# Sparsemax cross-attention and ffn on one core: three Newton rounds for the thresholds instead of four, members compared by row, and a rearranged end

## The chip, the cores and the metric

The kernel runs on one core of a Trainium2 chip. The time is that of the device, in microseconds; three runs of the kernel before gave 677.35, 680.38 and 681.27 us, median 680.38. One more execution was profiled; its trace is what is read here.

## What is computed

Eight batches of 100 queries and 722 context rows, model width 512, 16 heads of 32. The attention's weights are a sparsemax, not a softmax: in each row of scores a threshold tau is subtracted and what is negative is cut, with tau such that the rest sums to one.

```python
def sparsemax(x):
    x = x - max(x); zs = sort(x, descending)
    cssv = cumsum(zs) - 1.0
    k = count(zs > cssv / rho)                 # rho = 1, 2, ...
    tau = cssv[k - 1] / k
    return clip(x - tau, 0.0)

q, k, v = layernorm(x) @ Wq + bq, ctx @ Wk + bk, ctx @ Wv + bv      # 16 heads each
attn = sparsemax(q @ k.T * 32 ** -0.5)                              # 100 x 722 a head
x = x + (attn @ v) @ Wo + bo
real, imag = layernorm(x) @ cos(theta + theta_noise), layernorm(x) @ sin(phi + phi_noise)
x = x + sqrt(real ** 2 + imag ** 2)
```

## The kernel before

The work goes by half-batches: half i is heads 0 to 7 (i even) or 8 to 15 (i odd) of batch i // 2, 16 halves in all. A phase i does three things at once, on queues whose order is written out by hand: PE attends half i - 1 (`attend`: the tau matmuls L600, the weights L612, the mixing with v L583), computes the scores of half i + 1 (L558), and fills what is between with the projections of k, v and q, the output projection (L514) and the ffn (L531). ACT empties the PSUM rings. DVE finds the thresholds of half i. Each engine runs its own list in order and waits on semaphores.

DVE's list for a half: for each of its 8 heads 16 MAX8 (L952), one for each of 16 pieces of a row of 722 scores; each leaves the eight largest of its piece in `cand`, stored rank by rank (8 x 16 = 128 candidates a row). Then `thresholds` runs Newton's method on f(tau) = sum(max(x - tau, 0)) - 1 for all 8 heads and 100 rows together: 4 turns over 2, 4, 6 and 7 ranks (`RANKS`), in which the positive differences are summed (`f_sum`) and the members counted (`n_over`, by way of `over` and `fold`). The first two steps are stretched by 1.15 and 1.1. The last step is cut at zero from below.

Then the marks. `over` says which of the 128 candidates are at or above the last tau. PE sums over the 100 rows (`sum_flags`): `n_over` of the last turn minus the members of ranks 0 to 6, plus the members of rank 7 (whose piece may hold more than its eight largest). If that is over 0.5 for a head, the head is marked. In the next phase DVE reads the marks behind the fourth head (`read_flags`, L1060 to L1066) and, behind the fifth, `settle` branches on them. With no marks it raises `verified` at once. For each marked head it runs `refine` on the whole row of 722 scores: L1029, then twice the loop of `two_steps` (L995 to L1006), a test of the sums (L1013 to L1020), and, where a sum is still over 1 + 1e-5, up to 14 further such rounds. Then `split_again` (L1045 to L1053) and `verified`. PE waits for `verified` in `attend` ahead of the tau matmuls, and everything behind these on its list waits with it.

At the end of the last batch PE runs the mixes, the output projection, the transposed x and both halves of the ffn; ACT copies the projection to `att`, POOL adds the residual (`attended_x`), sums the squares (`sum_squares`) and adds the root (`y_of`).

Of the kernel before, what the change touches and what calls it, by code (L numbers as in the profile page):

```python
# [8 lines left out]
BF16 = mybir.dt.bfloat16  # L9
# [18 lines left out]
RANKS = (2, 4, 6, 7)  # L28
STRETCH = (1.15, 1.1, 1.0, 1.0)
ROUNDS_MORE = 14  # L30
TINY = 2.0 ** -20
# [14 lines left out]
def build_kernel(nc, x, ctx_in, Wq, bq, Wk, bk, Wv, bv, Wo, bo, theta, phi, theta_noise, phi_noise, out):  # L46
# [69 lines left out]
    with es:  # L116
# [35 lines left out]
        dif, over = sb("dif", [L, HH, PIECES * max(RANKS)]), sb("over", [L, HH, NCAND], BF16)  # L152
        fold = sb("fold", [L, HH, 2 + PIECES * max(RANKS) // 2], BF16)
        tau = sb("tau", [L, 2, HH])
        f_sum, step_t, n_over = (sb(n, [L, HH]) for n in ("f_sum", "step_t", "n_over"))
        zero = sb("zero", [L, 1])
        one_b, minus_b = sb("one_b", [L, 1], BF16), sb("minus_b", [L, 1], BF16)
# [10 lines left out]
        relu_row = dif[:, :, :].rearrange("p g n -> p (g n)")[:, 0:N]  # L168
        mask_row = over[:, :, :].rearrange("p g n -> p (g n)")[:, 0:N]
# [146 lines left out]
        def _(pool):  # L316
# [90 lines left out]
            for i in PHASES:  # L407
                b, odd = divmod(i, 2)
                attended = 0 <= i - 1 < NH
                if odd:  # L410
# [12 lines left out]
                    if 0 <= b - 1 < B:  # L423
                        sum_squares(b - 1)
                else:
# [13 lines left out]
                    if b > 0:  # L439
                        residual(b - 1)  # L440
                        attended_x(b - 1)
            y_of(B - 1)

        @block.tensor
        def _(pe):
# [90 lines left out]
            def sum_flags(i):  # L536
# [97 lines left out]
            for i in PHASES:  # L634
# [4 lines left out]
                if odd:  # L639
# [13 lines left out]
                    fill = chain(itertools.islice(queries, 3), x2, queries, ffn)  # L653
# [10 lines left out]
                else:  # L664
# [6 lines left out]
                    fill = chain(*[v_of(b, kc) for kc in range(KC)]) if b < B else iter(())  # L671
                    run(fill, 4)
                    for n, _ in enumerate(units):
                        run(fill, 2 if n == 0 else 1)
# [521 lines left out]
```

## Time and profile before

| | |
|---|---|
| runs, median of 3 | 680.38 us |
| profiled execution, its own time | 676.18 us |
| its span | 674.4 us |
| mean granted TensorE clock | 0.915 |
| PE, DVE, ACT, POOL busy | 85%, 85%, 56%, 28% |
| MAX8 on DVE (L952), 2048 instructions | 223.5 us |
| HBM read, written | 23.77 MB, 1.64 MB |

The page gives busy time by engine and by line; the chain of waits follows the end back through what released each step; the timeline lists instructions in order, with the idle time ahead of each and its releaser in square brackets; the table of stretches gives busy time and clock between two times. A granted clock of 1.00 is 2.4 GHz and 0.50 is 1.2 GHz. Times are in us from the start of the span.

### The profile page before, as it was taken

How to read it: one execution, taken by the hardware profiler on the slowest of the kernel's cores; microseconds unless marked ns; L12 is line 12 of the kernel's file. 1: busy time of each engine (PE TensorE's matmuls, PEld its weight loads, DVE VectorE, ACT ScalarE, POOL GpSimd, SP SyncE). 2: the span in 40 equal slices, each digit the busy share in tenths (PEclk: the TensorE clock that was granted, in tenths of full speed). 3: DMA queues.
4: the chain of work that ended last, by engine and by line, in shares of the span. 5: the costliest groups of instructions: out<-in, count | busy, mean ns of one | idle time of the engine just before them, and what ended most of it. 6: DMA issues, size and time to landing. Idle time of an engine off the chain costs nothing.

```text
span 674.4 us, 14485 instructions
## 1 busy us (share of the span) xinstructions
PE 571.3 (85%) x4648; PEld 336.7 (50%) x4648; DVE 573.3 (85%) x2900; ACT 378.0 (56%) x657; POOL 189.0 (28%) x239
## 2 busy tenths in 40 slices
PE   2686999999913999899999999991899999988675
PEld 1343665656502655565556555651556565645431
DVE  5699999978967999999999999995999999999400
ACT  3674568767511667566756676661466666554321
POOL 2711322332220250435133422342024431310301
PEclk9968987999965999999999999996899999996768
DMA  9863022302230103130323022302203020300000
GB/s 309 273 173 91 16 63 74 96 7 62 84 84 0 31 11 98 55 98 5 85 69 105 0 61 89 103 11 61 76 9 98 20 54 27 80 7 9 13 1 12
DMA packets 33506, 44.25 MB, mean 66 GB/s; under 512 B 8386, under 2 KB 26818, under 8 KB 33415
## 3 DMA queue, kind: packets, MB, share of 16 engines
q1 hardware_dynamic: 32332, 41.16, 21.4%
q10 hardware_dynamic: 1088, 2.10, 0.9%
q8 instruction: 37, 0.61, 0.4%
q14 instruction: 49, 0.39, 0.2%
HBM read 23.77 MB, written 1.64 MB: 38 GB/s over the span
## 4 chain that ended last, share of the span: by engine, by line
PE 49%; DVE 26%; issue 11%; ACT 7%; SPq 4%; DMA 2%; POOL 1%; DVEq 0%; POOLq 0%; ACTq 0%
PE ring L463 29%; DVE cand L952 7%; PE mix_bank L583 3%; PE ring L612 3%; DVE dif L966 3%; PE ring L514 3%; PE ring L558 3%; DVE f_sum L975 3%; SPq L255 3%; DVE over L969 3%; ACT S L692 3%; PE ring L531 2%; DVE n_over L977 2%; DVE dif L970 2%; PE ring L501 1%
## 5 line engine op out<-in xcount | busy, mean ns | idle before, releaser
L952 DVE MAX8 cand<-S 100x8 f32<-100x45 f32 (+1 forms) x2048 | 223.5, 195 | 2.1 <-issue 0.4
L463 PE MATMUL ring<-wv,ctx 128*121 128x512 f16 x576 | 154.5, 390 | 0.0
L463 PE MATMUL ring<-ctx,wk 128*128 128x361 f16 x768 | 125.7, 323 | 4.7 <-DVE ctx L1118 4.7
L817 ACT ACTIVATE pT<-ring 121x800 f32<-121x800 f32 x96 | 80.5, 839 | 72.3 <-PE ring L612 71.6
L692 ACT ACTIVATE S<-ring 100x722 f32<-100x722 f32 x128 | 95.5, 773 | 32.6 <-PE ring L558 32.6
L463 PEld LDWEIGHTS ring<-ctx,wk 128*128 128x128 f16 x768 | 75.1, 99 | 50.0 <-issue 7.1
L340 POOL TENSOR_TENSOR ctx<-ctx_f,ctx 128x484 f16<-128x484 f32 x42 | 51.5, 1225 | 149.8 <-ACT ctx L692 149.4
L463 PEld LDWEIGHTS ring<-wv,ctx 128*121 128x121 f16 x576 | 71.4, 136 | 34.0 <-issue 7.7
L348 POOL TENSOR_TENSOR ks<-k_f,ks 128x361 f16<-128x361 f32 x64 | 57.9, 905 | 79.6 <-ACT k_f L704 76.7
L558 PE MATMUL ring<-kst,qst 96*100 96x361 f16 x256 | 65.1, 348 | 11.5 <-DMA kst<-ks 8.9
L612 PEld LDWEIGHTS ring<-qst,kst 99*121 99x121 f16 x768 | 59.3, 147 | 29.7 <-issue 13.8
L700 ACT ACTIVATE ks<-ring,bk_c 128x361 f16<-128x361 f32 x64 | 36.0, 563 | 65.3 <-PE ring L463 65.3
L612 PE MATMUL ring<-qst,kst 99*121 99x100 f16 x768 | 64.3, 231 | 2.9 <-ACT qst L692 2.9
L583 PE MATMUL mix_bank<-pT,v 121*32 121x100 f32 x1536 | 56.8, 269 | 1.9 <-ACT aT L800 1.2
L558 PEld LDWEIGHTS ring<-kst,qst 96*100 96x100 f16 x256 | 30.8, 133 | 55.3 <-issue 21.5
L692 ACT ACTIVATE qst<-ring 96x800 f16<-96x800 f32 (+1 forms) x32 | 25.7, 829 | 49.6 <-PE ring L600 45.9
L966 DVE TENSOR_TENSOR dif<-cand,tau 100x256 f32<-100x256 f32 (+1 forms) x64 | 51.3, 801 | 2.2
L583 PEld LDWEIGHTS mix_bank<-pT,v 121*32 121x32 f32 x1536 | 34.0, 115 | 35.4 <-issue 30.7
L975 DVE TENSOR_REDUCE f_sum<-dif 100x8 f32<-100x256 f32 (+1 forms) x64 | 49.7, 777 | 0.0
L600 PE MATMUL ring<-ident,tt 100*3 100x100 f16 x128 | 9.5, 225 | 46.0 <-issue 42.3
L374 POOL TENSOR_TENSOR sq<-sq 100x512 f32<-100x512 f32 x8 | 10.1, 1264 | 112.9 <-ACT sq L782 112.9
L969 DVE TENSOR_SCALAR over<-dif 100x256 bf16<-100x256 f32 (+1 forms) x64 | 38.4, 601 | 2.2
(124 smaller groups left out, 722.9 us busy)
## 6 DMA issues: line engine op xcount, KB each, us to landing
kst<-ks SPq DMA_DIRECT2D x384, 45.1 KB, 1.9
ctx_f<-in_ctx SPq DMA_DIRECT2D x45, 242.0 KB, 2.9
xq<-in_x SPq DMA_DIRECT2D x8, 200.0 KB
xr<-in_x SPq DMA_DIRECT2D x8, 200.0 KB
out_y<-att SPq DMA_DIRECT2D x8, 200.0 KB
S<-in_L_xattn_Wk ACTq DMA_DIRECT2D x1, 1024.0 KB, 6.9
wq<-in_L_xattn_Wq ACTq DMA_DIRECT2D x1, 1024.0 KB, 11.4
wcos<-in_L_ffn_theta SPq DMA_DIRECT2D x1, 1024.0 KB, 10.4
```

What stands on the lines that cost most here:

```text
L340: pool.tensor_tensor(ctx2[:, 1, :, at], ctx_f[:, n % 3, :, :], ctx2[:, 0, :, at], ALU.subtract).then_inc(ctx_lo_ready, 1)
L348: pool.tensor_tensor(ks[:, n % 2, 1, at], k_f[:, u % 2, :], ks[:, n % 2, 0, at], ALU.subtract).then_inc(k_lo_ready, 1)
L463: last = nc.tensor.matmul(psum, lhs(c, i), w(c, j), start=(c == 0 and n == 0), stop=(c == DC - 1 and n == 2))
L558: last = nc.tensor.matmul(psum[0:L, half, 0:HALF], qst[0:3 * DH, b % 2, HH * part + h, :], kst[0:3 * DH, i % 3, h, half * HALF:(half + 1) ...
L583: last = nc.tensor.matmul(mix_ps[DH * j:DH * (j + 1), :], v[0:CK, i % 3, kc, DH * (G * g + j):DH * (G * g + j + 1)], pT[0:CK, st_unit(i, g ...
L612: last = nc.tensor.matmul(psum[0:CK, c, j * L:(j + 1) * L], kst[0:99, i % 3, G * g + j, kc * CK:(kc + 1) * CK], qst[0:99, b % 2, HH * part ...
L692: return nc.scalar.activation(dst, src, ACT.Copy, **kw)
L817: nc.scalar.activation(pT[0:CK, u % 3, :, :], src, ACT.Relu).then_inc(two_read, 1)
L952: last = nc.vector.max(pieces[:, h, :, n], S[0:L, HH * (i % 2) + h, cuts[n]:cuts[n + 1]])
L966: n = counted(nc.vector.tensor_tensor(dif[:, :, 0:E], cand[:, :, 0:E], t3.broadcast_to([L, HH, E]), ALU.subtract))
L969: n_mask = counted(nc.vector.tensor_scalar(over[:, :, 0:E], dif[:, :, 0:E], 0.0, None, ALU.is_ge))
L975: counted(nc.vector.reduce_sum(f_sum[:, :], dif[:, :, 0:E], AX))
```

## The change

Thresholds: three turns over 3, 6 and 7 ranks. The start is 0.9 of the old one plus a tenth of the row's largest score (`TOWARDS_MAX`, `top`). Only the second step is stretched, by 1.12, and then held to at most `top`. The last step is no longer cut at zero. The members are written as f32 zeros (raised to `TINY`) and ones beside the positive differences, and one TENSOR_REDUCE over both gives `f_sum` and `n_over`.

Marks: the members at the last tau are counted again (`n_still`), and `changed` is 1 for each row and head where this count is not the one that the last step used. PE sums `changed` and the members of rank 7; the seven matmuls with `minus_b` go.

End: the last output projection is issued in quarters, each as its part of `aT` is there; the ffn of batch 6 stands behind the mixes of half 14; for the last batch DVE adds projection and residual from PSUM (`last_x`), sums the squares and adds the root (`last_y`).

```diff
-RANKS = (2, 4, 6, 7)
-STRETCH = (1.15, 1.1, 1.0, 1.0)
+RANKS = (3, 6, 7)
+STRETCH = (1.0, 1.12)
+TOWARDS_MAX = 0.1
 ROUNDS_MORE = 14
-TINY = 2.0 ** -20
+TINY = 2.0 ** -32
...
+        dif = sb("dif", [L, 2, HH, PIECES * max(RANKS)])
+        over = dif[:, 1, :, :].bitcast(BF16)[:, :, 0:NCAND]
+        sums = sb("sums", [L, 2, HH])
+        f_sum, n_over = sums[:, 0, :], sums[:, 1, :]
...
             def o_of(b):
-                pe.wait_ge(aT_ready, DC * (b + 1))
                 for c in range(DC):
+                    pe.wait_ge(aT_ready, DC * b + c + 1)
...
             def sum_flags(i):
-                nc.tensor.matmul(flag_ps[:, :, PIECES], ones[:, :], n_over[:, :], start=True, stop=True)
-                for r in range(8):
-                    last = nc.tensor.matmul(flag_ps[:, :, 0:PIECES], (one_b if r == 7 else minus_b)[:, :],
-                                            marks[:, :, r, :], start=(r == 0), stop=(r == 7))
-                last.then_inc(flag_sum, 1)
+                nc.tensor.matmul(flag_ps[:, :, PIECES], ones[:, :], changed[:, :], start=True, stop=True)
+                nc.tensor.matmul(flag_ps[:, :, 0:PIECES], one_b[:, :], marks[:, :, 7, :], start=True,
+                                 stop=True).then_inc(flag_sum, 1)
...
             def thresholds(i, found):
+                counted(nc.vector.tensor_reduce(top[:, :], cand[:, :, 0:PIECES], AX, ALU.max))
+                n = counted(nc.vector.tensor_reduce(f_sum, cand[:, :, 0:PIECES], AX, ALU.add))
                 after(n)
-                n = counted(nc.vector.tensor_scalar(t, f_sum[:, :], -1.0, 1.0 / PIECES, ALU.add, ALU.mult))
+                n = counted(nc.vector.tensor_scalar(t, f_sum, -1.0, (1.0 - TOWARDS_MAX) / PIECES, ALU.add, ALU.mult))
+                after(n)
+                n = counted(nc.vector.scalar_tensor_tensor(t, top[:, :], TOWARDS_MAX, t, ALU.mult, ALU.add))
                 for turn, ranks in enumerate(RANKS):
...
-                    n_mask = counted(nc.vector.tensor_scalar(over[:, :, 0:E], dif[:, :, 0:E], 0.0, None, ALU.is_ge))
-                    n_dif = counted(nc.vector.tensor_scalar(dif[:, :, 0:E], dif[:, :, 0:E], 0.0, None, ALU.max))
-                    n_fold = counted(nc.vector.tensor_tensor(fold[:, :, 2:2 + E // 2], over[:, :, 0:E // 2],
-                                                             over[:, :, E // 2:E], ALU.add))
-                    counted(nc.vector.reduce_sum(f_sum[:, :], dif[:, :, 0:E], AX))
-                    n_count = counted(nc.vector.reduce_sum(n_over[:, :], fold[:, :, 0:2 + E // 2], AX))
+                    counted(nc.vector.tensor_scalar(member, above, 0.0, TINY, ALU.is_ge, ALU.max))
+                    n = counted(nc.vector.tensor_scalar(above, above, 0.0, None, ALU.max))
+                    n = counted(nc.vector.reduce_sum(sums[:, :, :], dif[:, :, :, 0:E], AX))
...
+                    if turn < len(RANKS) - 1 and STRETCH[turn] > 1.0:
+                        after(n)
+                        n = counted(nc.vector.tensor_tensor(t, t, top[:, :], ALU.min))
-                nc.vector.scalar_tensor_tensor(t, step_t[:, :], 0.0, t, ALU.max, ALU.add).then_inc(tau_ready, 1)
+                nc.vector.tensor_tensor(t, step_t[:, :], t, ALU.add).then_inc(tau_ready, 1)
                 dve.wait_ge(tau_ready, i + 1)
-                nc.vector.tensor_tensor(over[:, :, :], cand[:, :, :], t3.broadcast_to([L, HH, NCAND]),
-                                        ALU.is_ge).then_inc(flag_ready, 1)
+                n = counted(nc.vector.tensor_tensor(over[:, :, :], cand[:, :, :], t3.broadcast_to([L, HH, NCAND]), ALU.is_ge))
+                after(n)
+                n = counted(nc.vector.reduce_sum(n_still[:, :], over[:, :, 0:PIECES * max(RANKS)], AX))
+                after(n)
+                nc.vector.tensor_tensor(changed[:, :], n_still[:, :], n_over, ALU.not_equal).then_inc(flag_ready, 1)
...
+            def last_x():
+                dve.wait_ge(one_full, one["o", B - 1] + 1)
+                dve.wait_ge(one_read, one["o", B - 1])
+                dve.wait_ge(res_ready, B)
+                dve.wait_ge(y_ready, B - 1)
+                nc.vector.tensor_tensor(x1[:, :], ring1[0:L, one["o", B - 1] % 3, :], xr[:, :], ALU.add).then_inc(one_read, 1)
+
+            def last_y():
+                dve.wait_ge(one_read, seen1(("ffn", B - 1, 1)))
+                nc.vector.tensor_tensor(sq[:, 1, :], sq[:, 0, :], sq[:, 1, :], ALU.add).then_inc(sqsum_ready, 1)
+                dve.wait_ge(root_ready, B)
+                dve.wait_ge(stored, 16 * (B - 1))
+                nc.vector.tensor_tensor(att[:, :], x1[:, :], sq[:, 0, :], ALU.add).then_inc(y_ready, 1)
```

DVE's list in the last half, from the last Newton turn to the marks, before:

```order
L966 TENSOR_TENSOR dif<-cand,tau 100x896
L969 TENSOR_SCALAR over<-dif 100x8x112
L970 TENSOR_SCALAR dif<-dif 100x896
L972 TENSOR_TENSOR fold<-over 100x8x56
L975 TENSOR_REDUCE f_sum<-dif 100x8
L977 TENSOR_REDUCE n_over<-fold 100x8
L979 RECIPROCAL step_t<-n_over 100x8
L981 SCALAR_TENSOR_TENSOR step_t<-f_sum,step_t 100x8
L986 SCALAR_TENSOR_TENSOR tau<-step_t,tau 100x8
L988 TENSOR_TENSOR over<-cand,tau 100x1024
```

The same place now (`sums` holds both sums, `dif` both the differences and the members):

```order
L977 TENSOR_TENSOR dif<-cand,tau 100x896
L979 TENSOR_SCALAR dif<-dif 100x896
L980 TENSOR_SCALAR dif<-dif 100x896
L982 TENSOR_REDUCE sums<-dif 100x16
L984 RECIPROCAL step_t<-sums 100x8
L986 SCALAR_TENSOR_TENSOR step_t<-sums,step_t 100x8
L994 TENSOR_TENSOR tau<-step_t,tau 100x8
L996 TENSOR_TENSOR dif<-cand,tau 100x8x128
L998 TENSOR_REDUCE n_still<-dif 100x8
L1000 TENSOR_TENSOR changed<-n_still,sums 100x8
```

The fold and one of two sums are gone from a turn, and behind the final comparison stand a recount and the comparison by row, before the marks go to PE.

PE's list at the end, from the last marks on, before (L514 is the output projection, L531 the ffn):

```order
L531 MATMUL ring<-wsin,k_f 100x512 x4
L542 MATMUL mix_bank<-n_over,ones 1x8
L544 MATMUL mix_bank<-over,minus_b 1x8x16 x7
L544 MATMUL mix_bank<-over,one_b 1x8x16
L600 MATMUL ring<-ident,tt 3x100 x8
L612 MATMUL ring<-qst,kst 121x100 x16
...
L612 MATMUL ring<-qst,kst 121x100 x8
L583 MATMUL mix_bank<-pT,v 32x100 x16
L514 MATMUL ring<-wo,aT 100x512 x4
L487 MATMUL ring<-ident,sq 128x100 x4
```

And now (L518 is the output projection, L547 the marks of rank 7):

```order
L535 MATMUL ring<-wsin,k_f 100x512 x4
L546 MATMUL mix_bank<-changed,ones 1x8
L547 MATMUL mix_bank<-dif,one_b 1x8x16
L518 MATMUL ring<-wo,aT 100x512
L602 MATMUL ring<-ident,tt 3x100 x8
L518 MATMUL ring<-wo,aT 100x512
L614 MATMUL ring<-qst,kst 121x100 x16
...
L518 MATMUL ring<-wo,aT 100x512
L585 MATMUL mix_bank<-pT,v 32x100 x16
L518 MATMUL ring<-wo,aT 100x512
L491 MATMUL ring<-ident,sq 128x100 x4
```

Three quarters of the projection have moved ahead of the last mixes, the first of them ahead of the tau matmuls, which wait for `verified`; seven of the nine matmuls on the marks are gone.

## Rows read from the trace of the kernel before

**Rows 1.** The page, busy us, share of the span and instructions of each engine.
```profile
PE 571.3 (85%) x4648; PEld 336.7 (50%) x4648; DVE 573.3 (85%) x2900; ACT 378.0 (56%) x657; POOL 189.0 (28%) x239
```

**Rows 2.** Table of stretches: length, busy us by engine, PEclk, DMA share, GB/s.
```profile
142.04:238.58 96.54, 69.61 (x582) 41.47 (x582) 78.11 (x359) 45.02 (x82) 24.03 (x29) 0.86 0.17 46
238.58:307.85 69.27, 67.31 (x582) 39.93 (x582) 66.56 (x349) 45.02 (x82) 23.56 (x30) 1.00 0.23 64
...
446.40:531.44 85.04, 69.11 (x583) 40.78 (x582) 74.08 (x379) 45.04 (x82) 23.45 (x30) 0.90 0.19 52
...
213.00:218.50 5.50, 5.47 (x28) 3.65 (x29) 5.44 (x46) 1.67 (x2) 0.00 (x0) 0.53 0.00 1
```

**Rows 3.** List of waits over the whole span: total us, times, longest us.
```profile
PE ring L600 <- issue: 42.3, 3, 25.2
...
PE mix_bank L542 <- DVE over L988: 11.4, 6, 3.5
```

**Rows 4.** Groups of DVE's instructions over the whole span: the count in `two_steps`.
```profile
L995 DVE TENSOR_SCALAR_CACHE_REDUCE over<-dif 100x722 bf16<-100x722 f32 x6 | 5.4, 905 | 2.1 <-DVE dif L1006 1.3 <-DVE dif L1029 0.7
```

**Rows 5.** Timeline of DVE, 187 to 214 us, two heads refined: start, us, instruction.
```profile
187.61 1.32 DVE L1029 SCALAR_TENSOR_TENSOR dif<-S,tau,zero 100x722 f32<-100x722 f32 x1 [1.27 <-issue]
...
190.85 0.92 DVE L1005 TENSOR_TENSOR tau<-tau,delta 100x1 f32 x1
...
201.19 0.97 DVE L1029 SCALAR_TENSOR_TENSOR dif<-S,tau,zero 100x722 f32<-100x722 f32 x1 [3.81 <-remote]
...
209.54 0.14 DVE L1020 TENSOR_REDUCE again_i<-again_m 1x1 int32<-1x4 f32 x1
211.86 0.17 DVE L1045 TENSOR_SCALAR t_rest<-tau 100x8 f32<-100x8 f32 x1 [2.18 <-remote]
...
213.02 0.69 DVE L928 BATCH_NORM_STATS2 st<-xq 100x6 f32<-100x512 f32 x1 [0.15 <-DVE tt L1053]
```

**Rows 6.** Timeline of DVE, 461 to 473 us, one head refined.
```profile
461.65 0.97 DVE L1029 SCALAR_TENSOR_TENSOR dif<-S,tau,zero 100x722 f32<-100x722 f32 x1 [4.47 <-issue]
...
470.02 0.14 DVE L1020 TENSOR_REDUCE again_i<-again_m 1x1 int32<-1x4 f32 x1
472.67 0.17 DVE L1045 TENSOR_SCALAR t_rest<-tau 100x8 f32<-100x8 f32 x1 [2.50 <-remote]
```

**Rows 7.** Timeline of DVE, 390 to 411 us, thresholds of a regular half.
```profile
390.35 0.17 DVE L934 RECIPROCAL sd<-sd 100x1 f32<-100x1 f32 x1 [0.56 <-ACT sd L769]
...
396.36 0.41 DVE L975 TENSOR_REDUCE f_sum<-dif 100x8 f32<-100x256 f32 x1
...
401.79 0.96 DVE L966 TENSOR_TENSOR dif<-cand,tau 100x768 f32<-100x768 f32 x1
...
406.09 1.09 DVE L966 TENSOR_TENSOR dif<-cand,tau 100x896 f32<-100x896 f32 x1
407.22 0.63 DVE L969 TENSOR_SCALAR over<-dif 100x896 bf16<-100x896 f32 x1
...
408.60 1.08 DVE L975 TENSOR_REDUCE f_sum<-dif 100x8 f32<-100x896 f32 x1
409.60 0.63 DVE L977 TENSOR_REDUCE n_over<-fold 100x8 f32<-100x464 bf16 x1
...
410.90 1.23 DVE L988 TENSOR_TENSOR over<-cand,tau 100x1024 bf16<-100x1024 f32 x1
```

**Rows 8.** Timeline of PE, 412 to 413 us, the marks.
```profile
412.23 0.57 PE L544 MATMUL mix_bank<-over,minus_b 100*1 100x128 bf16 x7
412.64 0.23 PE L544 MATMUL mix_bank<-over,one_b 100*1 100x128 bf16 x1
```

**Rows 9.** Timeline of all engines, 646 to 672 us, the end.
```profile
646.62 6.19 PE L514 MATMUL ring<-wo,aT 128*100 128x512 f32 x8 [0.46 <-ACT aT L800]
...
653.57 1.26 POOL L369 TENSOR_TENSOR x<-att,xr 100x512 f32<-100x512 f32 x1 [18.74 <-issue]
...
668.13 1.26 POOL L374 TENSOR_TENSOR sq<-sq 100x512 f32<-100x512 f32 x1 [13.29 <-ACT sq L782]
...
670.19 1.26 POOL L379 TENSOR_TENSOR att<-x,sq 100x512 f32<-100x512 f32 x1 [0.80 <-ACT sq L786]
```

More of the change, by code:

```diff
@@ L151, in build_kernel @@
         cand = sb("cand", [L, HH, NCAND])
-        dif, over = sb("dif", [L, HH, PIECES * max(RANKS)]), sb("over", [L, HH, NCAND], BF16)
-        fold = sb("fold", [L, HH, 2 + PIECES * max(RANKS) // 2], BF16)
+        dif = sb("dif", [L, 2, HH, PIECES * max(RANKS)])
+        over = dif[:, 1, :, :].bitcast(BF16)[:, :, 0:NCAND]
         tau = sb("tau", [L, 2, HH])
-        f_sum, step_t, n_over = (sb(n, [L, HH]) for n in ("f_sum", "step_t", "n_over"))
+        sums = sb("sums", [L, 2, HH])
+        f_sum, n_over = sums[:, 0, :], sums[:, 1, :]
+        step_t, top = sb("step_t", [L, HH]), sb("top", [L, HH])
         zero = sb("zero", [L, 1])
-        one_b, minus_b = sb("one_b", [L, 1], BF16), sb("minus_b", [L, 1], BF16)
+        n_still, changed = sb("n_still", [L, HH]), sb("changed", [L, HH])
+        one_b = sb("one_b", [L, 1], BF16)
         bit_c, code, lost = (sb(n, [1, HH]) for n in ("bit_c", "code", "lost"))
@@ L167, in build_kernel @@
         st2, mv2, sd2 = sb("st2", [L, 6]), sb("mv2", [L, 2]), sb("sd2", [L, 2])
[L168 to L169 removed]
+        relu_row = dif[:, :, :, :].rearrange("p a g n -> p (a g n)")[:, 0:N]
+        mask_row = dif[:, 1, :, :].rearrange("p g n -> p (g n)").bitcast(BF16)[:, 0:N]
         marks = over[:, :, :].rearrange("p g (r n) -> p g r n", r=8)
@@ L652, in _ @@
                     ffn = ffn_of(b - 1) if 0 <= b - 1 < B else iter(())
-                    fill = chain(itertools.islice(queries, 3), x2, queries, ffn)
+                    idle = iter([None] * (0 if b + 1 < B else 2))
+                    fill = chain(itertools.islice(queries, 3), x2, queries, idle, ffn)
                     for n, _ in enumerate(units):
@@ L671, in _ @@
                     fill = chain(*[v_of(b, kc) for kc in range(KC)]) if b < B else iter(())
+                    attended_o = o_of(b - 1) if b > 0 else iter(())
                     run(fill, 4)
+                    if b == B:
+                        run(attended_o, 1)
                     for n, _ in enumerate(units):
                         run(fill, 2 if n == 0 else 1)
+                        if b == B and n in (0, 10):
+                            run(attended_o, 1)
                     weave(heads, fill, 1)
-                    if b > 0:
-                        run(o_of(b - 1), 4)
+                    run(attended_o, 4)
                     if i < NH:
@@ L963, in thresholds @@
+                after(n)
+                n = counted(nc.vector.scalar_tensor_tensor(t, top[:, :], TOWARDS_MAX, t, ALU.mult, ALU.add))
                 for turn, ranks in enumerate(RANKS):
                     E = PIECES * ranks
+                    above, member = dif[:, 0, :, 0:E], dif[:, 1, :, 0:E]
                     after(n)
-                    n = counted(nc.vector.tensor_tensor(dif[:, :, 0:E], cand[:, :, 0:E],
-                                                        t3.broadcast_to([L, HH, E]), ALU.subtract))
+                    n = counted(nc.vector.tensor_tensor(above, cand[:, :, 0:E], t3.broadcast_to([L, HH, E]), ALU.subtract))
@@ L1130, in _ @@
             nc.vector.memset(one_b[:, :], 1.0).then_inc(dve_const, 1)
-            nc.vector.memset(minus_b[:, :], -1.0).then_inc(dve_const, 1)
             for h in range(HH):
                 counted(nc.vector.memset(bit_c[:, h:h + 1], 2.0 ** h))
-            n = [counted(nc.vector.memset(again[:, :], 0.0)), counted(nc.vector.memset(zero[:, :], 0.0)),
-                 counted(nc.vector.memset(fold[:, :, 0:2], TINY))][-1]
+            n = [counted(nc.vector.memset(again[:, :], 0.0)), counted(nc.vector.memset(zero[:, :], 0.0))][-1]
             after(n)
@@ L1168, in _ @@
             settle(NH - 1)
+            last_x()
             ln2_stats(B - 1)
             ln2_apply(B - 1)
+            last_y()
 _INS = ["x", "ctx_1024", "L0_xattn_Wq", "L0_xattn_bq", "L0_xattn_Wk", "L0_xattn_bk", "L0_xattn_Wv", "L0_xattn_bv",
```

22 lines of the change are left out of this document (11 added, 11 removed).

## Prediction, made before the changed kernel was run

> **What bounds the kernel now.** The page says that PE and DVE are both busy for 85% of the span [rows 1], so I went on to equal stretches. In the table of stretches, a regular pair of half-batches takes 69.27 us, of which PE works 67.3 [rows 2]. DVE's column shows 66.6, but in its timeline it goes from one instruction to the next: the only wait that I find in such a pair is 0.56 us for a square root [rows 7]. So DVE's chain is the bound, and PE is just under it: over the whole span it waits only 11.4 us in 6 places for the marks (L542 behind L988) [rows 3].
>
> The second thing to see is what is not regular. Two pairs take 96.54 and 85.04 us instead of 69.27 [rows 2]. In the list of waits that is PE's 42.3 us before the tau matmuls (L600) [rows 3], and in DVE's timeline it is `refine`: two heads after half 3 [rows 5], one after half 10 [rows 6]. PE waits for `verified` before it attends, and DVE has its own four remaining heads and the next thresholds behind the refinement. So a refinement is added to the time in full: 96.54 - 69.27 = 27.3 us for two heads, 85.04 - 69.27 = 15.8 us for one. It is the only part of this kernel whose cost depends on the data, and the change alters the rule that calls it. That decides the prediction; the rest is small.
>
> **How many heads will be refined.** I applied both rules to the reference's own inputs: scores of all 8 x 16 heads x 100 rows, the eight largest of each of the 16 pieces, then the thresholds as the code has them. For the kernel before this gives 3 marked heads: half 3, heads 0 and 3, and half 10, head 6. That is what the trace shows, at the same halves: L1029 stands twice from 187 us and once at 461 us, each with two rounds of L995 (6 in all) and no further ones [rows 4, 5, 6]. So I trust the same working for the new rule, and it says 120 of 128 heads, 6 to 8 in each half.
>
> The reason can be followed. The new thresholds make three rounds, and the second step is stretched by 1.12, past the root; the last, unclamped step then goes back below the root and picks up members that the count of its own round did not have. In 367 of 12,800 rows (2.9%) the count after the last step is one or two larger than the count that the step used. The old mark was the difference of two sums over the 100 rows and saw only losses, and its last step was clamped at zero. The new mark compares row by row with `not_equal`, so one such row marks its head. With 2.9 such rows in 100, a head is left unmarked with a chance of about 0.971^100 = 5%, or some 7 of 128, which agrees with the 8 counted. The excess of the sum is small in these rows (1e-4 in the middle one), but no tolerance stands in the mark. After two rounds of `two_steps` all 120 heads come out within the limit, so the loop of up to 14 more is never entered.
>
> **Price of a pause, step by step.** From L1029 to the end of L1020, one head takes 470.16 - 461.65 = 8.5 us, and the second head at half 3 the same, 209.68 - 201.19 [rows 5, 6]; the first one took 9.8, its L1029 being 1.32 instead of 0.97 us and L1005 0.92 instead of 0.16. Behind a head come the load of `again_i`, the jump over the long loop and the loops over heads: 2.2 and 2.5 us to the end of the loops, 3.8 us to another head with two unmarked ones between [rows 5, 6]. Neighbouring marked heads do not occur before. The gap between them is bounded by 1.3 us (a load and the entry, before the first L1029) from below and 3.8 from above; I take 2.3, the tails' mean. Entry 1.3 and `split_again` 1.2 (to the next DVE work at 213.02) come once per half. For eight heads: 1.3 + 8 x (8.5 + 2.3) + 1.2 = 88.9 us. Over the kernel: 120 x 8.5 = 1020, 120 x 2.3 = 276, 16 x 2.5 = 40, 6 for unmarked heads jumped over, 10 for the first heads that meet POOL: 1352 us. With 1.3 us a gap it is 1232, with 3.8 it is 1532.
>
> On the jumps the Trainium skill (Advanced Engine Details and Errata, Control Flow Timing) gives about 108 ns for a compare-and-branch and 51 ns for a branch. The tails of 2.2 and 2.5 us in the trace are far above a handful of these, so the skill's figures alone would put the gap too low; by them, with some eight jumps, it would be about 0.8 us, and the sum some 180 us smaller. I go by the rows.
>
> **The thresholds themselves.** Start to start in the last turn of the old form [rows 7]: subtract 1.13, mark 0.54, clip and fold 0.84, sum 1.00, count and the three small ones 1.30, together 4.81 us from 406.09 to 410.90. The turn of 768 takes 4.30 (401.79 to 406.09), those of 512 and 256 in the same timeline 3.3 and 2.3, the first mean 0.53 and the final comparison 1.23: 16.5 us. New, from the same rows: `fold` and the bf16 count go, one sum over twice the width stands for both. The f32 sums run at 1.04 ns an element (0.41 for 256, 1.08 for 896 [rows 7]), so 1792 elements are 2.05 with the gap, and a turn of 896 is 1.13 + 0.54 + 0.66 + 2.05 + 0.24 + 0.20 + 0.20 = 5.0. The turn of 768 with its `min` is 4.7, that of 384 is 2.85, the head with `top` 0.9, the comparison 1.26, the recount of 896 1.1 and `not_equal` 0.2: 16.0 us. Four rounds to three gives only 0.45 us a half, since what is saved in turns goes into the wider sum and the recount: -7 us over 16. If the member form (is_ge, max, f32 out) does not run at the rate of the bf16 mark (0.63 for 896) but at that of the subtraction (1.09), 0.9 a half is lost instead of 0.45 won: +8. I take -7, since input and width are those of L969.
>
> The seven minus matmuls of L544 (0.41 us of PE a half, 412.23 to 412.64 [rows 8]) go too. In a regular pair that would lower PE's 67.3 to 66.5, but with a pause in each half PE has spare time: 0.
>
> **The end.** From the last mix, a whole output projection (L514, 6.2 us for 8 records, at the lower clock), ACT's copy 0.6, POOL's sum 1.26, and at the very end two POOL sums of 1.26 with the root between [rows 9]. With three of the four quarters issued earlier, some 4 us of L514 leave the end; one DVE sum read from PSUM for copy and POOL sum saves about 1.2, two DVE sums of some 0.7 (at the subtraction's rate, 0.96 for 768 [rows 7]) for POOL's save 1.2. `last_y` waits for nothing that ACT and PE do not already finish there. The ffn of batch 6 moves behind the mixes, into time in which PE waits for L988 anyway [rows 3]: nothing. The last half's own pause (8 heads) stands before all of it and is counted above. -6 us.
>
> **Sum.** Against the profiled execution's 676.18 us: -43.1 (the old pauses) + 1352 - 7 - 6 = 1972. The median of the runs is 4.2 above that execution: about 1976, and I say 1980.
>
> **The rivals.**
> Faster: the marks stay rare. If the rows counted by me did not differ on the chip, only heads with a member of rank 7 would be marked, two by the same working (half 3 head 3, half 10 head 6). Then 676.2 - 7 - 6 - (43.1 - 31.6) = 652, or 655 us in the median: the change would do what its rounds and its end suggest. For it speaks only that the excess is small; against it, the rule's exact count of old marks [rows 4]. It decides from under about 5 marked heads. 5%.
> Jumps cost more in some halves: before the one head at half 10 there were 4.5 us, before the first at half 3 only 1.3 [rows 5, 6]; if 3.2 us more fell on each head in 4 of 10 halves, +155: 2130 us. 
> PE becomes the bound: the granted clock reads 0.53 in the 5.5 us after the 25 us pause, so 1.2 GHz nearly throughout, and 0.86 over the whole pair [rows 2]. PE's half is 33.6 us of work at 2.4 GHz, of which some 27 come after the pause; if it stayed at 1.2 GHz for these, the half would end some 17 us later than DVE's chain, +270: 2250. Against it: with 25 us of pause the pair's 0.86 leaves PE at the full clock for most of the rest. 4%.
> The loop of more rounds is entered: 14 turns of at least a 2.2 us load and jump are 31 us a head; in one head of ten that is +370, 2350. The worked rule says none. 3%.
> Forecast as summed: 74%, its own range 1850 to 2160 (the gap's 1.3 and 3.8, the member's rate).
>
> **The numbers.** 80% range: 1860 to 2200, which takes in the second rival. What a measurement of this kernel can tell from no change is about 0.5%. Faster 0.05, same 0.01, slower 0.94.
>
> **What the profile would show.** Right: the first step of `refine` about 120 times, its rounds 240; PE's wait before the tau matmuls near 1300 us; each pair about 240 us long; the first step of `refine` in a half some 10 us after the final comparison. The old `fold` gone, the sum near 2.0 us for 1792. Wrong: a handful of refinements (my count is wrong), more than two rounds a head (the limit is missed), a head's chain above 8.5 us, or gaps far from 2.3 us.

## The result, and the profile after

The changed kernel takes 1978.29 us in the median of 4 executions (1977.56 to 1978.90), against 679.2 us (677.35 to 681.27) for the kernel before beside it: a ratio of 2.912, 95% interval 2.903 to 2.922. The forecast was 1980 us. The profiled execution has a span of 1975.8 us and a mean granted clock of 0.642; before it was 674.4 and 0.915.

Busy time, from the page of the changed kernel:

```profile
PE 593.0 (30%) x4536; PEld 346.5 (18%) x4536; DVE 1407.7 (71%) x5736; ACT 377.6 (19%) x656; POOL 186.2 (9%) x236
```

Against [rows 1], DVE has worked 834 us more, in nearly twice as many instructions; PE, ACT and POOL did about the same work. DVE bounds this span and still is idle for 29% of it, 568 us, where it was idle for 101; so over a third of the loss must be waits on DVE. The list of waits of the same execution has it (total us, times, longest):

```profile
PE ring L602 <- issue: 1342.0, 16, 92.7
...
DVE dif L1040 <- remote: 236.9, 104, 3.9
...
DVE dif L1040 <- issue: 47.4, 16, 6.1
...
DVE t_rest L1056 <- DVE again_i L1031: 23.2, 16, 1.5
```

L602 is the line of the tau matmuls, L600 in [rows 3]: 42.3 us in 3 places have become 1342 in all 16 halves. L1040 is the first step of `refine`. It comes behind another marked head 104 times, with 2.28 us of idle time each, and as the first of a half 16 times. The groups of instructions give the number of heads:

```profile
L1006 DVE TENSOR_SCALAR_CACHE_REDUCE dif<-dif 100x722 bf16<-100x722 f32 x240 | 217.3, 906 | 92.4 <-DVE dif L1017 64.9 <-DVE dif L1040 27.6
L1040 DVE SCALAR_TENSOR_TENSOR dif<-S,tau,zero 100x722 f32<-100x722 f32 x120 | 123.8, 1032 | 284.3 <-remote 236.9 <-issue 47.4
```

120 heads, and 240 = 2 x 120 counts: two rounds a head, never more. In [rows 4] the count stood 6 times. Counted half by half, the first steps are 8, 6, 7, 7, then 8 in seven halves, and 7, 6, 7, 8, 8: the numbers of the rule worked out ahead, half for half.

One half in DVE's timeline of the changed kernel, from the thresholds to the split:

```profile
886.89 0.29 DVE L967 TENSOR_REDUCE top<-cand 100x8 f32<-100x128 f32 x1
...
896.50 0.63 DVE L979 TENSOR_SCALAR dif<-dif 100x896 f32<-100x896 f32 x1
...
897.70 2.02 DVE L982 TENSOR_REDUCE sums<-dif 100x16 f32<-100x1792 f32 x1
...
901.65 1.09 DVE L998 TENSOR_REDUCE n_still<-dif 100x8 f32<-100x896 bf16 x1
902.77 0.17 DVE L1000 TENSOR_TENSOR changed<-n_still,sums 100x8 f32<-100x8 f32 x1
...
914.44 0.97 DVE L1040 SCALAR_TENSOR_TENSOR dif<-S,tau,zero 100x722 f32<-100x722 f32 x1 [2.18 <-issue]
...
924.00 0.14 DVE L1031 TENSOR_REDUCE again_i<-again_m 1x1 int32<-1x4 f32 x1
926.02 0.97 DVE L1040 SCALAR_TENSOR_TENSOR dif<-S,tau,zero 100x722 f32<-100x722 f32 x1 [1.87 <-remote]
...
934.47 0.14 DVE L1031 TENSOR_REDUCE again_i<-again_m 1x1 int32<-1x4 f32 x1
937.06 0.97 DVE L1040 SCALAR_TENSOR_TENSOR dif<-S,tau,zero 100x722 f32<-100x722 f32 x1 [2.45 <-remote]
...
947.50 0.97 DVE L1040 SCALAR_TENSOR_TENSOR dif<-S,tau,zero 100x722 f32<-100x722 f32 x1 [1.83 <-remote]
...
959.09 0.97 DVE L1040 SCALAR_TENSOR_TENSOR dif<-S,tau,zero 100x722 f32<-100x722 f32 x1 [3.00 <-remote]
...
999.39 0.14 DVE L1031 TENSOR_REDUCE again_i<-again_m 1x1 int32<-1x4 f32 x1
1000.99 0.17 DVE L1056 TENSOR_SCALAR t_rest<-tau 100x8 f32<-100x8 f32 x1 [1.45 <-DVE again_i L1031]
```

From 914.44 to 1000.99 nothing but eight refinements. A head takes 934.61 - 926.02 = 8.6 us; the first takes 9.7. The gaps follow the nesting of the loops over heads in `settle`: about 1.85 us to the second head of a pair, 2.45 to the next pair, 3.00 to the next four.

What PE makes of it is in the table of stretches (length, busy us by engine, granted clock, DMA share, GB/s):

```profile
903.00:1000.00 97.00, 12.45 (x72) 7.29 (x70) 66.77 (x283) 8.75 (x17) 9.65 (x12) 0.59 0.06 16
...
1001.00:1028.00 27.00, 25.70 (x231) 15.95 (x232) 25.79 (x94) 16.78 (x32) 4.81 (x4) 0.91 0.08 20
1028.00:1036.00 8.00, 8.00 (x45) 4.27 (x44) 7.90 (x68) 3.45 (x8) 4.88 (x5) 1.00 0.00 0
```

PE stands through the pause: of its 12.45 us of work in the first row 9.0 lie ahead of 912 us. The granted clock averages 0.59 in that row, near its lower level (1.2 GHz, 0.50), and is back at 1.00 (2.4 GHz) before the half's work is done. The low mean of 0.642 is a consequence of the pauses.

The end, timeline of the changed kernel, to set beside [rows 9]:

```profile
1938.81 0.83 PE L602 MATMUL ring<-ident,tt 100*3 100x100 f16 x8 [89.73 <-issue]
...
1943.42 0.90 PE L585 MATMUL mix_bank<-pT,v 121*32 121x100 f32 x16 [0.19 <-ACT pT L824]
...
1954.53 2.03 PE L518 MATMUL ring<-wo,aT 128*100 128x512 f32 x2 [0.46 <-ACT aT L807]
...
1956.60 0.69 DVE L1109 TENSOR_TENSOR x<-ring,xr 100x512 f32<-100x512 f32 x1 [17.94 <-PE ring L518]
...
1970.75 0.69 DVE L1113 TENSOR_TENSOR sq<-sq 100x512 f32<-100x512 f32 x1 [11.34 <-ACT sq L789]
```

A quarter of the projection (2.03 us) is left behind the last mix in place of 6.19, and DVE's sums take 0.69 in place of POOL's 1.26. From the tau matmuls to the end of the span it is 37.0 us; before, 41.3.

### The profile page after: what moved, and what is told of

It is laid out like the page before. It is cut to its first block, busy times and chain, and to the rows that moved or that the text cites. A ratio compares the mean times of both kernels' runs of the same rounds, so it can differ in the third digit from the quotient of the medians.

```text
span 1975.8 us, 20109 instructions
## 1 busy us (share of the span) xinstructions
PE 593.0 (30%) x4536; PEld 346.5 (18%) x4536; DVE 1407.7 (71%) x5736; ACT 377.6 (19%) x656; POOL 186.2 (9%) x236
## 4 chain that ended last, share of the span: by engine, by line
issue 71%; PE 25%; ACT 2%; SPq 1%; DMA 1%; DVE 0%; POOL 0%; POOLq 0%; ACTq 0%; DVEq 0%
PE ring L467 11%; PE ring L535 3%; PE ring L614 2%; PE mix_bank L585 2%; PE ring L505 2%; PE ring L560 2%; PE ring L518 1%; SPq L259 1%; ACT S L699 1%; PE ring L602 1%; SPq L263 0%; PE ring L571 0%; DMA S<-in_L_xattn_Wk 0%; PE ring L491 0%; DMA kst<-ks 0%
## 5 line engine op out<-in xcount | busy, mean ns | idle before, releaser
L602 PE MATMUL ring<-ident,tt 100*3 100x100 f16 x128 | 13.2, 280 | 1342.0 <-issue 1342.0
L1040 DVE SCALAR_TENSOR_TENSOR dif<-S,tau,zero 100x722 f32<-100x722 f32 x120 | 123.8, 1032 | 284.3 <-remote 236.9
L1006 DVE TENSOR_SCALAR_CACHE_REDUCE dif<-dif 100x722 bf16<-100x722 f32 x240 | 217.3, 906 | 92.4 <-DVE dif L1017 64.9
L602 PEld LDWEIGHTS ring<-ident,tt 100*3 100x3 f16 x128 | 9.8, 113 | 1348.4 <-issue 1348.4
L1017 DVE SCALAR_TENSOR_TENSOR dif<-dif,delta,zero 100x722 f32<-100x722 f32 x240 | 231.4, 964 | 0.0
L467 PE MATMUL ring<-wv,ctx 128*121 128x512 f16 x576 | 163.2, 407 | 0.0
L1029 DVE TENSOR_REDUCE again_m<-againT 1x1 f32<-1x32 f32 x480 | 83.7, 174 | 15.4
L982 DVE TENSOR_REDUCE sums<-dif 100x16 f32<-100x768 f32 (+2 forms) x48 | 75.6, 1576 | 1.6
L614 PEld LDWEIGHTS ring<-qst,kst 99*121 99x121 f16 x768 | 65.7, 158 | 32.6 <-issue 24.6
L358 POOL TENSOR_TENSOR qn<-sq,qn 100x512 f16<-100x512 f32 x7 | 8.8, 1257 | 658.9 <-ACT sq L699 658.9
L614 PE MATMUL ring<-qst,kst 99*121 99x100 f16 x768 | 68.5, 241 | 0.9 <-ACT qst L699 0.9
```

Source lines behind the costliest of these rows:

```text
L467: last = nc.tensor.matmul(psum, lhs(c, i), w(c, j), start=(c == 0 and n == 0), stop=(c == DC - 1 and n == 2))
L614: last = nc.tensor.matmul(psum[0:CK, c, j * L:(j + 1) * L], kst[0:99, i % 3, G * g + j, kc * CK:(kc + 1) * CK], qst[0:99, b % 2, HH * part ...
L982: n = counted(nc.vector.reduce_sum(sums[:, :, :], dif[:, :, :, 0:E], AX))
L1006: nc.vector.tensor_scalar(mask_row, relu_row, 0.0, None, ALU.is_gt, ALU.add, accum_out=count[:, :]).then_inc(fix, 1)
L1017: nc.vector.scalar_tensor_tensor(relu_row, relu_row, delta[:, :], zero[:, :].broadcast_to([L, N]), ALU.subtract, ALU.max, accum_out=new_su ...
L1029: nc.vector.reduce_max(again_m[0:1, q:q + 1], againT[32 * q:32 * q + 1, :], AX).then_inc(fix, 1)
```

## The experiments

There were ten runs of nine kernels, each with runs of the kernel before on the same chip.

**Marks for losses only.** The changed kernel with another comparison. Rows whose count rose are not refined; their sum is over 1 by up to 2.5e-3, as worked out on the inputs.

```diff
-nc.vector.tensor_tensor(changed[:, :], n_still[:, :], n_over, ALU.not_equal)
+nc.vector.tensor_tensor(changed[:, :], n_still[:, :], n_over, ALU.is_lt)
```

> The changed kernel with one operator exchanged: a row is marked only where the members at the last tau are fewer than the last step used (is_lt instead of not_equal). Every instruction stays in its place and at its size; what is left out is the refinement of heads whose rows have gained a member. By the rule worked out on the inputs, 2 heads are marked (half 3 head 3, half 10 head 6). Theory (the time is the number of marked heads): the changed kernel's 1978 less 1352 of pauses is 626, plus two pauses of 15.8 is 658 us, some 20 under the kernel before. Rival (the new thresholds or the new end cost by themselves, the pauses only hide it): 680 us or more with as few pauses. Second rival (the marks are raised by something else than gained rows): still over 1900 us.

Measured: 647.67 us (646.97 to 648.48), ratio 0.955, interval 0.952 to 0.958. From its list of waits, and a regular pair of halves from its table of stretches:

```profile
PE ring L602 <- issue: 31.0, 2, 15.6
...
233.35:301.17 67.82, 66.39 (x569) 39.20 (x567) 64.94 (x328) 44.93 (x82) 23.32 (x29) 1.00 0.23 66
```

Two heads are refined instead of 120, and 1331 us are gone: refining the heads with gained rows is the whole loss. The time is 10 us below what I expected, so small terms of the sum were too small. The pair is 67.82 us where [rows 2] had 69.27, -1.45 and not -0.9; and from the last reading of the marks to the end of the span it takes 33.0 us where it took 42.8.

**Every head marked.** The kernel before, untouched but for the constant that `lost` is compared with.

```diff
-nc.vector.scalar_tensor_tensor(code[:, :], lost[:, :], 0.5, bit_c[:, :],
+nc.vector.scalar_tensor_tensor(code[:, :], lost[:, :], -1000.0, bit_c[:, :],
```

> The kernel before with every head marked (the comparison of the marks is with -1000 instead of 0.5), nothing else changed. Theory: 679 less the old pauses of 43 is 636, plus 128 heads at 8.5 + 2.3 and 16 halves at 2.5 is 1422: 2058 us, with the thresholds, marks and end of before. Rival (part of the 1300 us comes from the change's own instructions): clearly under 2000 us. Rival (TensorE's lower clock after each pause becomes the bound): over 2100 us.

Measured: 2055.11 us (2053.66 and 2056.56). Its group of the first step:

```profile
L1029 DVE SCALAR_TENSOR_TENSOR dif<-S,tau,zero 100x722 f32<-100x722 f32 x128 | 133.2, 1040 | 281.3 <-remote 231.8 <-issue 37.5 <-DVE again_i L1020 12.0
```

Old thresholds, old end, old code of the refinement, and it is slower still than the changed kernel; 2058 us was expected. The loss needs nothing of the change but the number of marks.

**No stretch.** The changed kernel with plain Newton steps.

```diff
-STRETCH = (1.0, 1.12)
+STRETCH = (1.0, 1.0)
```

> The changed kernel with no stretch at all (1.0, 1.0). By the worked rule 81 rows change, all of them losses, and 66 heads are marked, 2 to 7 in a half. Theory: 626 + 66 x 10.8 + 16 x 2.5 + 46 for 54 more unmarked heads jumped over + 8 = 1425 us. It also tells whether the stretch of 1.12 is the whole cause: if three rounds were enough without it, the time would be near 660 us; the theory says they are not.

Measured: 1429.92 us (1427.28 and 1432.55). Its group of the first step:

```profile
L1040 DVE SCALAR_TENSOR_TENSOR dif<-S,tau,zero 100x722 f32<-100x722 f32 x66 | 70.0, 1060 | 202.7 <-remote 151.1 <-issue 51.5
```

66 heads, as the rule worked out for these steps says, and 5 us from the expected time. By the working on the inputs the changed rows are all losses here, so marking losses only would not help: without the stretch three rounds are too few. With 2, 66 and 120 heads the time rises at a nearly constant price: (1429.92 - 647.67) / 64 = 12.2 us for each of the first 64 heads, in which nearly every half gets its entry and tail, and (1978.29 - 1429.92) / 54 = 10.2 for each of the rest.

**Comparison by row in the kernel before.** Its four turns, its thresholds and its end stay; only the marks are made as in the change (and `TINY` is 2 to the -32).

```diff
-nc.tensor.matmul(flag_ps[:, :, PIECES], ones[:, :], n_over[:, :], start=True, stop=True)
+nc.tensor.matmul(flag_ps[:, :, PIECES], ones[:, :], changed[:, :], start=True, stop=True)
-for r in range(8):
-    last = nc.tensor.matmul(flag_ps[:, :, 0:PIECES], (one_b if r == 7 else minus_b)[:, :],
-                            marks[:, :, r, :], start=(r == 0), stop=(r == 7))
+nc.tensor.matmul(flag_ps[:, :, 0:PIECES], one_b[:, :], marks[:, :, 7, :], start=True, stop=True)
...
+n = counted(nc.vector.reduce_sum(n_still[:, :], over[:, :, 0:PIECES * max(RANKS)], AX))
+after(n)
+nc.vector.tensor_tensor(changed[:, :], n_still[:, :], n_over[:, :], ALU.not_equal).then_inc(flag_ready, 1)
```

> The kernel before, four rounds and old sums, with only the marks compared by row (recount, not_equal, two matmuls instead of nine; TINY 2^-32 so that the counts are whole). By the worked rule the same 3 heads are marked. Theory: the pauses stay at 43; DVE does 1.3 us more in each half and is the bound, PE 0.4 less: 679 + 16 x 1.3 = 700 us. Rival (comparing by row alone brings the marks): over 1000 us. Rival (PE's list is the bound and DVE's addition is hidden): 673 to 680 us.

Measured: 687.79 us (687.18 to 690.41), ratio 1.014, interval 1.010 to 1.018. PE's wait for the marks:

```profile
PE mix_bank L543 <- DVE changed L991: 21.4, 8, 4.8
```

The first step of `refine` stands 3 times in its trace, as before, so the rival of many marks falls. The comparison as such costs 9 us, not the 20 of my 700 us. From one final comparison to the next, regular pairs did become 2.1 to 2.6 us longer, as expected. But the half ahead of the first pause (half 3) took 36.1 us where it had taken 40.5, and the first two halves together only 1.3 us more; what bounds these halves is not shown.

**A fourth turn.** The changed kernel with its own comparison and one more plain turn.

```diff
-RANKS = (3, 6, 7)
-STRETCH = (1.0, 1.12)
+RANKS = (3, 6, 7, 7)
+STRETCH = (1.0, 1.12, 1.0)
```

> The changed kernel with a fourth, plain turn over 7 ranks (RANKS 3, 6, 7, 7). By the rule worked out on the inputs the fourth step starts from below the root and gains no member: 2 heads are marked instead of 120, with the same comparison by row. Theory (the marks come from a last step that goes back over the root, not from the comparison itself): the time is that of the run that marks losses only, 647.7, plus a turn of 896 in each half, 5.0 us x 16 = 80 at most where VectorE bounds: 715 to 728. Rival (the comparison not_equal itself is true for other reasons, such as a count that differs in form): some 120 heads stay, and it is near 2050.

Measured: 737.34 us (736.03 to 740.41). Its groups, the first step of `refine` and the sum of 1792:

```profile
L1040 DVE SCALAR_TENSOR_TENSOR dif<-S,tau,zero 100x722 f32<-100x722 f32 x3 | 2.9, 971 | 8.9 <-issue 8.9
...
L982 DVE TENSOR_REDUCE sums<-dif 100x16 f32<-100x1792 f32 x32 | 64.6, 2020 | 1.1
```

Three heads, not 120 and not two: the rule worked out misses one (in half 2). On the inputs, half 2 has the candidate that lies nearest to its last threshold, 6e-8 away, where the nearest of any other half is 3e-7 away; a difference in rounding there would be enough, but no run shows that this is the row. The half with its pause took 53.8 us from one final comparison to the next, where 38.2 and a turn of 5.0 would be 43.2; these 10.6 us lift the time over the expected 715 to 728. The rival falls: the same `not_equal`, on steps that end on the root, marks almost nothing.

**Marks of rank 7 alone.** The kernel for losses only, without recount and comparison, without the matmul on `changed` and without its column in the sum that DVE reads (`lost`). No row is refined because its count changed.

```diff
-n = counted(nc.vector.reduce_sum(n_still[:, :], over[:, :, 0:PIECES * max(RANKS)], AX))
-nc.vector.tensor_tensor(changed[:, :], n_still[:, :], n_over, ALU.is_lt).then_inc(flag_ready, 1)
```

> The changed kernel without recount and comparison: only members of rank 7 mark a head (2 heads by the worked rule, as with losses only). It leaves out the refinement of all rows whose count changed. VectorE has 1.3 us less in each half (the recount 1.1, the comparison 0.2). If VectorE's chain alone bounds, 647.7 - 20 = 628. But PE works 66.4 of 67.8 us in a pair, so theory says PE becomes the bound after 1.4 us a pair: 647.7 - 8 = 640, with PE's column in the table of stretches at the length of the pair and a wait of DVE appearing. Rival: no gain at all, since something else sets the pair.

Measured: 646.72 us (645.38 to 647.47), 1 us under the kernel for losses only, and their intervals overlap (0.950 to 0.956 and 0.952 to 0.958). Two regular pairs of its table of stretches, and of PE's timeline the tau matmuls and a mix of the last half:

```profile
289.42:356.05 66.63, 66.25 (x565) 39.05 (x564) 63.96 (x324) 45.00 (x82) 23.24 (x29) 1.00 0.24 67
356.05:422.76 66.71, 66.33 (x565) 39.12 (x564) 64.03 (x324) 45.08 (x83) 23.18 (x29) 1.00 0.24 67
```
```profile
609.41 0.52 PE L601 MATMUL ring<-ident,tt 100*3 100x100 f16 x8 [2.44 <-POOLq L402]
...
612.93 0.90 PE L584 MATMUL mix_bank<-pT,v 121*32 121x100 f32 x16 [0.19 <-ACT pT L823]
```

The time says "no gain", the profile says otherwise. PE now works 66.3 of 66.7 us: it has become the bound, as expected, and the last marks are read at 605.97 us instead of 612.17. But from there to the end of the span it takes 39.4 us instead of 33.0, and the 6.2 us are gone. Of these 6.4 us, 1.9 lie ahead of the tau matmuls, which here wait 2.44 us and there 0.53; the other 4.5 lie behind them. From 616 to 626 us the granted clock was 0.50: 0.90 us for 16 mixing matmuls, where the kernel for losses only has 0.55.

**The end alone.** The kernel before with the three changes at the end: quarters, the moved ffn, and the sums on DVE (the lines of `o_of`, `idle`, `last_x` and `last_y` of the change's diff); and the same without the move.

```diff
-fill = chain(itertools.islice(queries, 3), x2, queries, ffn)
+idle = iter([None] * (0 if b + 1 < B else 2))
+fill = chain(itertools.islice(queries, 3), x2, queries, idle, ffn)
```

> The kernel before with only the new end: quarters of the last output projection, the ffn of batch 6 behind the mixes of half 14, last_x and last_y on VectorE; thresholds and marks as before. My prediction's own term for the end was -6 us (some 673). The run with marks for losses only showed 30.1 us from the last marks read to the end against 40.1 before, so the theory now says -10: 669. From the last L1067-like read of the marks to the end it should be 30 us and the last mixes should run at 0.55 us per 16 instead of 0.90. Rival: part of those 10 us came from the shorter regular phases ahead of the end, then the stretch stays near 34 and the time near 673.

> As end_only, but the ffn of batch 6 stays where it was, ahead of the last marks instead of behind the mixes of half 14. Theory: the moved ffn keeps PE busy right ahead of the last attention, so that it runs at the full clock; without the move the last mixes are back at 0.90 us per 16, the end costs 4 us more than in end_only, some 673. Rival: the move does nothing and all of the gain comes from quarters and VectorE's sums: same time as end_only.

Measured: with the move 668.74 us in the median of six, ratio 0.986, interval 0.983 to 0.990; without it 671.2 us (664.1 to 676.8), ratio 0.983, interval 0.980 to 0.987. The ratios leave out a sixth execution with the move, of 1933 us, and the two longest without it, of 675.5 and 676.8; the medians of what is left are 667.2 and 668.3. The execution of 1933 us has a granted clock of 1.00, where every kernel with many refined heads has 0.64 to 0.70, so it is something else; it left no trace and its cause is open. So the end alone is worth some 10 us, and the move cannot be told from nothing. The profiled executions do differ. PE's marks and a mix of the last half, with the move:

```profile
629.62 0.19 PE L542 MATMUL mix_bank<-n_over,ones 100*1 100x8 f32 x2 [0.79 <-DVE over L993]
...
635.56 0.55 PE L583 MATMUL mix_bank<-pT,v 121*32 121x100 f32 x16 [0.57 <-ACT pT L822]
```

and without it:

```profile
633.61 0.20 PE L542 MATMUL mix_bank<-n_over,ones 100*1 100x8 f32 x2 [3.51 <-DVE over L993]
...
641.97 0.90 PE L583 MATMUL mix_bank<-pT,v 121*32 121x100 f32 x16 [0.19 <-ACT pT L822]
```

Where PE had waited 3.51 us before the marks, the last half ran at the lower clock (37.2 us from the reading of the marks to the end of the span, against 31.6 with the move). The expectation's 30.1 and 40.1 us do not come out of the traces: from the first instruction on the marks it is 33.0 for losses only and 42.8 before, with the same difference. That suggested a theory of the clock, with a spread of 13 us over the executions against it, so I tried it where the spread is small.

**Does the move keep the clock?** The kernel for losses only, without the move and with it, in one group. The edit is the line of `idle` above.

> The kernel whose marks are set for losses only (rows whose count rose stay unrefined), with the two matmuls of batch 6's ffn that the change had put behind the mixes of half 14 back between these mixes. Nothing else on any engine moves. In the profile of end_no_move PE's wait before the last marks was 3.51 us and the last attention ran at the lower clock (the stretch after the marks 0.50), with the move 0.79 us and 1.00; but over the runs the two were not told apart (668.7 and 671.2 us, spread 664 to 677). Theory: the wait of PE in front of the last marks brings the clock down for the last attention; here it is 4.8 instead of 2.05 us, the last mixes take 0.90 per 16 instead of 0.55, and the time is 5 to 6 us longer, 653. Rival: the clock at the end falls or not by chance from execution to execution; then both have the same median within 1 us.

> Marks for losses only, once more, beside losses_no_move on the same chip (rows whose count rose stay unrefined). Theory: 647.7 as before, with a spread below 2 us, so that a difference of 5 us from its neighbour is seen. Rival (chance sets the clock at the end): some of its executions near 653.

Measured: without the move 645.36 us (644.10 to 648.04), with it 648.27 (646.69 to 648.79). I had expected 653 without it; the sign is the other way round, and the intervals of the two ratios overlap (0.950 to 0.956 and 0.953 to 0.959). The table of stretches, without the move:

```profile
610.00:616.00 6.00, 3.84 (x31) 1.97 (x31) 1.66 (x5) 2.34 (x4) 4.74 (x8) 1.00 0.11 31
616.00:626.00 10.00, 7.21 (x132) 4.54 (x132) 1.58 (x4) 4.90 (x8) 0.00 (x0) 1.00 0.01 4
```

and with it:

```profile
610.00:616.00 6.00, 3.42 (x16) 1.25 (x15) 3.23 (x6) 1.90 (x3) 3.89 (x8) 0.90 0.00 0
616.00:626.00 10.00, 8.98 (x149) 6.21 (x148) 0.00 (x0) 5.64 (x9) 1.03 (x1) 0.89 0.08 23
```

The clock is higher without the move, so the move does not keep it up. PE's wait before the marks is 2.05 us in both profiles, not the 4.8 that I expected, so whether a long wait there brings the clock down was not tested by this pair. From the reading of the marks to the end of the span it takes 30.8 us without the move and 33.0 with it. One half earlier the profiles of all kernels without long pauses say the same: the mixes of half 14 begin at 0.90 us for 16 and come back to 0.55 before they are through in the four without the move (before, comparison by row, and the two without the move above), and in none of the five with it, where PE has no ffn matmuls between them. What remains is a bound on the move's worth, between nothing and a loss of 3 us here, and an open question: what decides at which clock the last half runs.

## Why the prediction was right, point by point

**The number of heads.** 120, exactly, with the same number in every half. It was the step on which all else hung, and the cheapest to get wrong from a diff: one comparison with another operator. It could be trusted because the same working gave the old marks of [rows 4], and its account of the marks fits the runs: all 367 changed rows worked out are gains, and they mark nothing when only losses count. The two runs with other rules (66 heads worked out and 66 found, 2 worked out and 3 found) show how far such a working goes: it is sound in the mass, and can miss a single head.

**A head and its gap.** 8.6 us for the chain in nearly every row where the forecast said 8.5, 8.74 in the mean with the slower first ones (1049 us for the 120, where the forecast has 1030), and 236.9 / 104 = 2.28 for the gap where it said 2.3. The gap was taken from tails of another kind (to the end of the loops), and the measured 1.85, 2.45 and 3.00 lie around them; that their mean came out at 2.3 is partly luck. The few branches at the Trainium skill's 108 and 51 ns (Advanced Engine Details and Errata, Control Flow Timing) do not give it: even the shortest gap, 1.7 us in the last half, is over twice the 0.8 us worked out from them.

**Entry and tail.** Entry 47.4 / 16 = 3.0 us on average, said 1.3, some 27 us too few: in the single rows it is 1.2 to 2.4 us in ten halves and 4.2 to 6.1 in six; the tail 23.2 / 16 = 1.45, said 2.3, some 14 too many. All pauses together, from the entry to the next work behind the split, came to 1375 us in the timeline (1049 for the chains, 237 for the gaps, 23 for the tails, 47 for the entries, 18 for the splits) against 1352.

**No further rounds, and PE's clock.** 240 counts for 120 heads. The clock is low in the pause and returns within the half: 0.91 from 1001 to 1028 us, 1.00 from there. PE is not the bound; that rival would have shown as DVE waiting for PE, and the only long such wait is one of 17.9 us in the last half.

**The thresholds.** From 886.89 to 902.94 it is 16.05 us, said 16.0, and the member form runs at the rate of the old mark, 0.63 us for 896, so the alternative falls (its 0.9 a half would have been 14 us over 16 halves, not the 8 of the prediction). The old thresholds take 17.3 us in the half of [rows 7], undisturbed 16.4, said 16.5. The rest is one mark that took 0.84 us longer than the same instruction in other halves (0.43), while POOL worked; in the timeline of the kernel before:

```profile
397.93 1.43 POOL L354 TENSOR_TENSOR qn<-sq,qn 100x512 f16<-100x512 f32 x1 [6.86 <-ACT sq L692]
398.38 1.27 DVE L969 TENSOR_SCALAR over<-dif 100x512 bf16<-100x512 f32 x1
399.57 0.41 DVE L970 TENSOR_SCALAR dif<-dif 100x512 f32<-100x512 f32 x1
```

So the term was mis-sized: it compared undisturbed with undisturbed. Over the 16 halves the thresholds take 280.5 us before and 268.8 in the changed kernel, -11.7 and not -7, since POOL stands in the long pauses and nine halves run at the undisturbed 16.05. In the kernel for losses only POOL works beside them as before, and there they take 280.7 us: nothing is saved, a regular pair has 18.4 + 16.8 where it had 17.3 + 18.1. That its pair is 1.45 us shorter all the same comes from elsewhere: fewer of DVE's other instructions are stretched (its instruction on the marks, L1062 before, takes 0.15 us and not 0.43), and the waits for the square root are 0.4 and not 0.7 us. That POOL's neighbourhood makes the difference is likely by these rows, and no run took it away.

**The end.** -4.3 us in the changed kernel, said -6: the quarters and DVE's sums do what was worked out, but PE comes out of a pause and all of the last half runs at 0.90 us for 16 matmuls, as it did before. With the last half at 0.55 the same end is 10 to 11 us shorter than before (33.0 and 31.6 us from the marks, against 42.8: the kernels for losses only and the end alone), with it at 0.90 only 5.6 (37.2, the end without the move). I had priced it at one clock and called the moved ffn nothing; nothing or a small loss is what its two pairs of runs say.

**The sum.** 1975.8 - 674.4 = 1301.4 us in the profiled executions. From the parts: 1374.6 - 43.1 - 11.7 - 4.3 = 1315.5, 14 us too many, so the pauses are not added in full. Some 9 of the 14 are waits of DVE that the kernel before has and the changed one mostly has not: for the square root 7.3 us and now 2.1, for the marks 4.1 and now 0.4. The rest is not traced. The forecast's parts gave 1296. Its errors (+23 for the pauses, -5 for the thresholds, +2 for the end, -14 for what the pauses hide) cancel, so the agreement of the totals to 2 us is luck; the number of heads and the price of one are not.

**The rivals.** Marks that stay rare (655 us) is what the kernel for losses only turned out to be, at 647.7: the arithmetic of that rival was right within 8 us, the condition was not met. Costlier jumps: what had spoken for them, 4.5 us before one head and 1.3 before another [rows 5, 6], is real and shows again in the entries, but once a half and not at each head; between heads it is never over 3.9 us.

## What to carry to other kernels

A test that sends work to a slow path has a rate, and that rate is the price of any change to the test: work it out on the data, on the old rule first, where the trace can confirm it. `not_equal` on counts also catches harmless changes; here a comparison for losses alone avoids the refinements and keeps what the rest of the change brings, and the kernel for losses only without the moved ffn (645.4 us) beats the one before by 4.7% (interval 4.4 to 5.0), if an excess of 2.5e-3 in a row sum, as worked out on the inputs, can be borne. When a saving vanishes from the time, measure stage by stage before giving up on it: 6 us were won in the pairs and lost again at the end.

## What the runs showed that I had not expected

- The clock at the end moves the whole by some 5 us. In the profiles of the kernels without long pauses the last half began at 0.90 us for 16 mixing matmuls where PE had idled 3.51 to 5.54 us before the marks (before, the end without the move, the comparison by row, a fourth turn) or 2.44 us before the tau matmuls (marks of rank 7 alone), and at 0.55 where it had idled 0.79 or 2.05 us before the marks (the end with the move, the three profiles for losses only). All nine fit, but these are coincidences of profiles, not a rule that an experiment confirmed.
- A DVE instruction beside a working POOL took three times as long as the same one in other halves (1.27 and 0.43 us). In the profile before, 39 single DVE instructions took at least 0.3 us longer than their like, 24 us in all, and every one of them overlaps one of POOL's; of the 48 TENSOR_REDUCE that overlap one, none is longer.
- The way from one pass of the refinement to the next costs two to three vector steps of 722 elements (0.91 us each): mostly 1.85 to 3.0 us, 237 us in the changed kernel.
